# First attention's last four groups written out among the dense mixture's first blocks

## The reference

```python
h = _L0_tok_ref(x, L0_tok_w, L0_tok_b, 16)
h = h + _L0_attn_ref(_layernorm(h), ...)
h = h + _L0_ffn_ref(_layernorm(h), ...)
...
def _attention(x, w_qkv, w_proj, b_proj, ln_gamma, ln_beta):      # 8 heads of 16
    ...
    attn = jax.nn.softmax(jnp.einsum('bhnd,bhmd->bhnm', q, k) * SCALE, axis=-1)
    out = jnp.einsum('bhnm,bhmd->bhnd', attn, v)
    ...
    out = jnp.einsum('bnc,dc->bnd', out, w_proj) + b_proj
    y = x + out
    return (y - mean) / jnp.sqrt(var + 1e-05) * ln_gamma + ln_beta
...
# _L0_ffn_ref: every token goes through all 8 experts (128 -> 512 -> 128)
leaf_probs = _leaf_probs(flat_x, rw, rb)          # 7 sigmoids in a tree, 8 products
h = jnp.einsum('nd,edh->neh', flat_x, w1) + b1[None]
h = jax.nn.gelu(h, approximate=False)
y = jnp.einsum('neh,ehd->ned', h, w2) + b2[None]
out = jnp.einsum('ned,ne->nd', y, leaf_probs)
```

## Time and profile before

| | us |
|---|---|
| median of three runs | 1234.58 |
| the profiled execution | 1236.1 |
| its span, the time in which instructions ran | 1234.3 |
| PE busy in the span | 1098.2 (89%) |
| DVE, ACT, POOL busy | 904.1, 845.1, 526.2 |
| last probabilities to the start of up(5), 161.6 to 201.5 | 39.9 |
| in it PE busy | 31.87 |

### The profile page before, as it was taken

How to read it: one execution, slowest core, us unless ns; L and a number is a source line. 1 busy time by engine, 2 the same in 40 slices (tenths; PEclk the granted TensorE clock), 3 DMA queues, 4 the chain that set the end, 5 groups by cost and what they waited for, 6 DMA issues and landing times. The chain is left out here.

```text
span 1234.3 us, 29279 instructions
## 1 busy us (share of the span) xinstructions
PE 1098.2 (89%) x8508; PEld 910.6 (74%) x8508; DVE 904.1 (73%) x2770; ACT 845.1 (68%) x2821; POOL 526.2 (43%) x885
## 2 busy tenths in 40 slices
PE   8999979999998999887388599998899899869996
PEld 5778857888887788776288477786678688657884
DVE  0488847999976889956565488886899788755774
ACT  1498858888885555557243378887788499846995
POOL 0379864444304278855252653323342011034552
PEclk9999989999999999988599689999999999959997
DMA  7300002322210000001522200000333100024441
GB/s 293 96 2 3 2 1 63 110 71 65 65 43 23 1 2 1 2 1 38 195 61 50 63 14 2 11 2 2 115 113 113 34 3 2 2 80 122 131 130 36
DMA packets 50824, 66.68 MB, mean 54 GB/s; under 512 B 8100, under 2 KB 30904, under 8 KB 50552
## 3 DMA queue, kind: packets, MB, share of 16 engines
q1 hardware_dynamic: 44552, 53.39, 14.2%
q0 software_dynamic: 4432, 6.59, 2.1%
q10 hardware_dynamic: 1696, 4.98, 1.0%
HBM read 58.32 MB, written 6.71 MB: 53 GB/s over the span
## 5 line engine op out<-in xcount | busy, mean ns | idle before, releaser
L495 DVE TENSOR_TENSOR f_parts<-T,f_parts 128x512 fp32r<-128x512 f32 (+1 forms) x240 | 181.7, 796 | 21.1 <-ACT f_parts L479 19.6
L471 ACT ACTIVATE T<-quad_bank,f_b1s 128x512 f32<-128x512 f32 (+1 forms) x240 | 150.5, 648 | 43.2 <-PE quad_bank L442 34.3
L442 PE MATMUL quad_bank<-XP,f_wp 128*128 128x512 f32 (+1 forms) x720 | 165.3, 373 | 1.1 <-ACT T L471 1.1
L442 PEld LDWEIGHTS quad_bank<-XP,f_wp 128*128 128x128 f32 x720 | 125.6, 188 | 26.4 <-ACT T L471 1.4
L479 ACT ACTIVATE f_parts<-T 128x512 fp32r<-128x512 f32 (+1 forms) x240 | 132.7, 593 | 0.0
L954 ACT ACTIVATE a_late<-quad_bank,a_shift 108x108 f32<-108x108 f32 x352 | 119.1, 363 | 2.7 <-DVE a_shift L1022 2.4
L455 PE MATMUL bank<-f_parts,f_wp 128*128 128x512 f32 (+1 forms) x480 | 116.7, 379 | 4.7 <-DVE XT L504 2.0
L455 PEld LDWEIGHTS bank<-f_parts,f_wp 128*128 128x128 f32 x480 | 85.4, 192 | 23.5 <-DVE a_late L524 2.8
L384 POOL TENSOR_TENSOR f_wp<-f_ws,const 128x512 fp32r<-128x512 f32 (+1 forms) x32 | 31.0, 968 | 122.3 <-DMA f_ws<-in_f_w 53.9
L954 ACT ACTIVATION_READ_ACCUMULATOR a_late<-quad_bank,a_shift 108x1 f32 x352 | 77.2, 219 | 0.0
L765 POOL TENSOR_TENSOR a_ve<-a_mv,const 108x1 f32<-108x1 f32 x44 | 8.3, 189 | 152.1 <-DVE a_mv L1079 152.0
(11 more groups left out here) (470 smaller groups left out, 3105.9 us busy)
## 6 DMA issues: line engine op xcount, KB each, us to landing
a_late<-f_gates SPq DMA_DIRECT2D x64, 256.0 KB, 3.2
a_wqk<-in_a_wqk SPq DMA_DIRECT2D x24, 256.0 KB, 2.5
f_ws<-in_f_w SPq DMA_DIRECT2D x16, 256.0 KB, 3.8
pats<-in_patches SPq DMA_DIRECT2D x5, 648.0 KB, 10.7
pats<-in_patches ACTq DMA_DIRECT2D x5, 648.0 KB, 14.8
a_late<-f_gates SPq DMA_DIRECT2D x16, 128.0 KB, 3.6
f_w1a<-in_f_w SPq DMA_DIRECT2D x1, 2048.0 KB, 11.4
f_w2a<-in_f_w SPq DMA_DIRECT2D x1, 2048.0 KB, 16.2
```

Of the source, the lines that this page charges most:

```text
L442: mm = pe.matmul(self.m.quad_bank[:, q % 4, 0:w], self.wp[0][:, e % 2, a, c * 128:(c + 1) * 128], self.xp[:, b, t0:t0 + w], start=((a, b) ...
L471: act.activation(self.full[:, q % 4, 0:w], self.m.quad_bank[:, q % 4, 0:w], self.func, bias=self.b1s[:, e * self.chunks + c:e * self.chunk ...
L495: dve.tensor_tensor(self.lo[:, q % self.ring, 0:w], self.full[:, q % 4, 0:w], self.hi[:, q % self.ring, 0:w], ALU.subtract).then_inc(self. ...
```

## The change

The last steps of PE, ACT and DVE, from G+4 on, are replaced by one list each, `last_groups`; POOL keeps its steps. In them:

- up(0) and up(1) are cut in halves, and the turn of group 17 and the output matmul of group 21 stand between the halves of up(0), the turn of 18 between those of up(1), 19 behind down(0), 20 and 21 behind up(2).
- the turns of groups 17, 18, 19 and 21 go to PSUM bank 1, that of 20 to bank 0.
- ACT calls GELU once on one column (`first_gelu`) before its first real GELU, so that the table load stands there; `high(17)` is behind two GELUs.
- DVE adds group 21 to `yt` and does the layer norms of 20 and 21 between the low parts; `low(17)` no longer stands ahead of the add.
- the six last router tiles stand together behind down(1); the logits are taken in DVE's turn of block 2.
- the gates are made in DVE's turn of block 2 (`gates_at` = 2) and not of block 0, PE turns them behind down(3) and not down(2), ACT copies them behind block 4 and not block 3.

```diff
...
 
-    def __init__(self, nc, m, ctx, sem, name, io, bias, func, experts, chunks, gates, room, lead, aside=None):
-        self.aside = aside
+    def __init__(self, nc, m, ctx, sem, name, io, bias, func, experts, chunks, gates, room, lead, aside=None, gates_at=0):
+        self.aside, self.gates_at, self.turn_at = aside, gates_at, 1 + lead + gates_at // 2
         if aside is not None:
...
 
-    def up(self, pe, i):
+    def up(self, pe, i, chunks=None):
         e, n, t0, w = self.block(i)
...
             pe.wait_ge(self.x_split, self.groups_in((t0 + w) // 128))
-        for c in range(self.chunks):
+        for c in chunks or range(self.chunks):
             q = i * self.chunks + c
...
 
-    def lows(self, dve, i):
+    def lows(self, dve, i, chunks=None):
         e, n, t0, w = self.block(i)
-        for c in range(self.chunks):
+        for c in chunks or range(self.chunks):
             q = i * self.chunks + c
...
             self.down(pe, i)
-            if i == 1 + self.lead:
+            if i == self.turn_at:
                 turn_gates()
...
             self.hidden(act, i)
-            if i == 1 + 2 * self.lead:
+            if i == self.turn_at + self.lead:
                 act.wait_ge(self.gt_psum, 1)
...
 
-    def vector(self, dve, done):
+    def vector(self, dve, done, between={}):
 
...
             ins.then_inc(self.h_done, 1)
-        dve.wait_ge(self.lg_ready, 2)
-        self.gates_first(dve)
         for i in range(self.last):
             e, n = divmod(i, nb)
+            if i in between:
+                between[i]()
+            if i == self.gates_at:
+                dve.wait_ge(self.lg_ready, 2)
+                self.gates_first(dve)
             if done <= i + self.lead < self.last:
...
                 self.raw(dve, n)
-                if n < len(self.gates_last):
-                    self.gates_last[n](dve)
-                if n == len(self.gates_last) - 1:
+                k = n - self.gates_at
+                if 0 <= k < len(self.gates_last):
+                    self.gates_last[k](dve)
+                if k == len(self.gates_last) - 1:
                     dve.drain()
...
     joined = lambda eng, step, depth: [step(t, t % 2) for t in range(G + 8)]
-    run = joined if follow is not None or channel_stats is not None else steps
-    turned_in = lambda t: [] if follow is None or t < 9 else [t - 9] if t < G + 5 else [G - 4, G - 3] if t == G + 5 else [t - 8]
-    turned_by = lambda t: max(0, t - 8) if t < G + 5 else t - 7
+    to_last_value = lambda eng, step, depth: [step(t, t % 2) for t in range(G + 4)]
+    run = to_last_value if follow is not None else joined if channel_stats is not None else steps
+    turned_in = lambda t: [] if follow is None or t < 9 else [t - 9]
+    turned_by = lambda t: max(0, t - 8)
     with ExitStack() as ctx:
...
         lg_at = m.quad_bank[:, 3, tiles * P:512]
+        first_gelu = sb("first_gelu", [128, 1]) if follow is not None else None
         routed_by = lambda t: mix.tiles_of(turned_by(t - 1))
...
                         mix.normalise(pool, t - 7)
-            run(pool, step, depth)
+            (joined if mix is not None else run)(pool, step, depth)
             if mix is not None:
...
                     pe.wait_ge(v_ready, min(G, t - 3))
-                    if t > G + 3:
-                        pe.wait_ge(y_done, min(G, t - 5))
                     mix.turn(pe, g, turn_at(i))
...
                     mm.then_inc(o_psum, 1)
-                if mix is not None:
-                    after_step(t)
 
-            def after_step(t):
-                if t == G + 3:
-                    pe.wait_ge(exps, 2 * G)
-                    pe.wait_ge(mix.lg_ready, 1)
-                    mix.up(pe, 0)
-                if t == G + 4:
-                    mix.up(pe, 1)
-                if t == G + 5:
-                    mix.route(pe, early_tiles, 14, qkbank[0], early_tiles)
-                    mix.down(pe, 0)
-                if t == G + 6:
-                    mix.route(pe, 14, 16, qkbank[0], early_tiles)
-                    mix.up(pe, 2)
-                if t == G + 7:
-                    mix.route(pe, 16, NT, qkbank[0], early_tiles)
-                    mix.down(pe, 1)
+            def last_groups():
+                pe.wait_ge(exps, 2 * G)
+                mix.up(pe, 0, (0, 1))
+                mix.turn(pe, G - 5, qkbank[0][:, 0:P])
+                pe.wait_ge(o_done, G)
+                pe.wait_ge(y_done, G - 1)
+                pe.wait_ge(mix.x_split, G - 5)
+                pe.matmul(xbank[0:P, 0:D], oT[:, :], wo[:, :], start=True, stop=True).then_inc(y_psum, 1)
+                pe.wait_ge(mix.lg_ready, 1)
+                mix.up(pe, 0, (2, 3))
+                mix.up(pe, 1, (0, 1))
+                pe.wait_ge(mix.x_split, G - 4)
+                mix.turn(pe, G - 4, qkbank[0][:, 0:P])
+                mix.up(pe, 1, (2, 3))
+                mix.down(pe, 0)
+                pe.wait_ge(mix.x_split, G - 3)
+                mix.turn(pe, G - 3, qkbank[0][:, 0:P])
+                mix.up(pe, 2)
+                pe.wait_ge(y_done, G)
+                mix.turn(pe, G - 2, xbank[:, 0:P])
+                pe.wait_ge(mix.x_split, G - 2)
+                mix.turn(pe, G - 1, qkbank[0][:, 0:P])
+                mix.down(pe, 1)
+                mix.route(pe, early_tiles, NT, qkbank[0], early_tiles)
             run(pe, step, depth)
             if mix is not None:
+                last_groups()
                 mix.tensor(pe, 3, 2)
...
                     exponentials(t - 3, q, 1)
-                for c in range(mix.chunks if mix is not None else 0):
-                    if t in (G + 3, G + 5):
-                        mix.gelu(act, (t - G - 3) // 2, c)
-                    if t in (G + 4, G + 6):
-                        mix.gelu_high(act, (t - G - 4) // 2, c)
+
+            def last_groups():
+                act.activation(first_gelu[:, :], m.one, mix.func)
+                mix.gelu(act, 0, 0)
+                mix.gelu(act, 0, 1)
+                mix.high(act, G - 5, qkbank[0][:, 0:P], G - 4)
+                mix.gelu(act, 0, 2)
+                mix.gelu(act, 0, 3)
+                for c in range(4):
+                    mix.gelu_high(act, 0, c)
+                mix.high(act, G - 4, qkbank[0][:, 0:P], G - 3)
+                for c in range(4):
+                    mix.gelu(act, 1, c)
+                mix.high(act, G - 3, qkbank[0][:, 0:P], G - 2)
+                for c in range(4):
+                    mix.gelu_high(act, 1, c)
+                for c in range(4):
+                    mix.gelu(act, 2, c)
+                mix.high(act, G - 2, xbank[:, 0:P], G - 1)
+                mix.high(act, G - 1, qkbank[0][:, 0:P], G)
+                for c in range(4):
+                    mix.gelu_high(act, 2, c)
+                mix.hidden(act, 3)
             run(act, step, depth)
             if mix is not None:
-                mix.hidden(act, 2)
+                last_groups()
                 mix.gates_middle(act, mix.lg_ready)
-                mix.scalar(act, 3)
+                mix.scalar(act, 4)
 
...
                     dve.tensor_tensor(oT[:, :], o_at, recT[:, :], ALU.mult).then_inc(o_done, 1)
-                if mix is not None and t in (G + 4, G + 6):
-                    mix.lows(dve, (t - G - 4) // 2)
+
+            def stats_of(g):
+                dve.wait_ge(h_done, g + 1)
+                mix.stats(dve, g)
+
+            def scaled(g):
+                dve.wait_ge(post_rstd, g + 1)
+                dve.tensor_scalar(yt[:, g % 2, :], yt[:, g % 2, :], mvb[:, g % 2, 0:1], rstdb[:, g % 2, :],
+                                  ALU.subtract, ALU.mult).then_inc(post_normed, 1)
+
+            def last_groups():
+                g = G - 1
+                dve.wait_ge(y_psum, G)
+                dve.wait_ge(xres_ready, G)
+                dve.wait_ge(h_done, g - 1)
+                dve.tensor_tensor(yt[:, g % 2, :], m.XN[:, bass.ts(g, D)], xbank[0:P, 0:D], ALU.add).then_inc(y_done, 1)
+                mix.low(dve, G - 5, qkbank[0][:, 0:P], G - 4)
+                dve.wait_ge(y_done, G)
+                dve.bn_stats(bnb[:, g % 2, :], yt[:, g % 2, :]).then_inc(post_stats, 1)
+                dve.drain()
+                dve.bn_aggr(mvb[:, g % 2, :], bnb[:, g % 2, :]).then_inc(post_stats, 1)
+                scaled(G - 2)
+                stats_of(G - 3)
+                mix.lows(dve, 0, (0, 1))
+                scaled(G - 1)
+                mix.lows(dve, 0, (2, 3))
+                stats_of(G - 2)
+                mix.low(dve, G - 4, qkbank[0][:, 0:P], G - 3)
+                stats_of(G - 1)
+                mix.lows(dve, 1)
+                mix.low(dve, G - 3, qkbank[0][:, 0:P], G - 2)
+
+            def last_turned():
+                mix.low(dve, G - 2, xbank[:, 0:P], G - 1)
+                mix.low(dve, G - 1, qkbank[0][:, 0:P], G)
             run(dve, step, depth)
-            dve.wait_ge(y_done, G)
             if mix is not None:
```

(8 more changed lines are left out.)

## The result

**The changed kernel takes 1226.63 us (median of 20 runs, 1220.89 to 1230.78) against 1234.53 us (20 runs, 1228.32 to 1241.58) in the same comparison: a ratio of 0.993, interval 0.9915 to 0.9946.** That is 7.9 us, 0.64%, inside the 1% that was called no change. Two later comparisons on other chips gave 0.9921 (0.9894 to 0.9949) and 0.9944 (0.9916 to 0.9972). The forecast was 8.9 us and 1225.7. The profiled execution took 1230.08 us, its span 1228.3, mean clock 0.938; that of before 1236.1, 1234.3 and 0.938.

What follows compares the result with a forecast made beforehand. It took the seam to lose PE time by waits and half clock, the mixture behind being PE-bound. Up(5) 10.6 us sooner less 1.7 for the clock gives 8.9: 1234.58 - 8.9 = 1225.7 us, range 1221.5 to 1232.

Steps and rivals of the forecast that it cites:

- What bounded the kernel: Seam loses PE time by standing still and lower clock; mixture behind is PE-bound and keeps the gain; at most 13.8 us.
- POOL's wait for the layer norm goes: Last groups: layer norm of group 20 done near 165.5 us, so POOL's wait of 2.51 us goes.
- POOL as the engine that is never idle: Last groups: POOL's steps set the chain; XN of group 21 at 174.5 to 177.9 us, taken as 177.
- One gap of PE, of 3 us: Ahead of the turns of groups 20 and 21: one gap of 0.5 to 3.9 us stays, taken as 3.
- the signs that I named: Profile checks, among them half clock at most once in the seam, up(5) at 188 to 193 us; wrong if after 195.
- The clock, 1.7 us: Behind PE's remaining gap: a short fall to 1.2 GHz costs 1.7 us, ends 0 and 3.4.
- Table load: ACT's early GELU call: GELU can begin 1.28 us sooner, less one short call; contained in the chain, not added.
- Routing at nothing: Seam: the six router tiles cost PE the same where they stand.
- gates at nothing: Seam and after: ACT's 2.77 us wait goes, PE has work meanwhile; later gates covered at no cost before expert 2.
- Contention of expert 1's splits at nothing in the seam: Block 2's low parts beside POOL's splits: 3.4 us more on DVE, taken as 0 for PE, ends 0 and 3.
- my third rival: Behind the seam: stretched low parts and a longer clock fall give back 2 to 6 us; 1229 to 1232.5; chance 0.16.
- the fourth rival: Blocks 5 to 8: DVE becomes the mixture's bound, 14.3 us lost against 8.9 won; 1240.0 us; chance 0.04.

Runs made afterwards that it cites:

- g10: Changed kernel with down(1)'s high and low parts moved into PE's gap, ahead of the turns of groups 20 and 21: 1239.73 us, ratio 0.9924 to the kernel before.
- e3: Changed kernel with the layer norm of group 20 ahead of the add of group 21 on DVE: 1236.33 us, ratio 0.989 to the kernel before.
- e1: Kernel before the change with only the gates made, turned and copied later: 1245.46 us against 1248.95, ratio 0.998.
- e2: Changed kernel with its gates one block earlier: 1240.37 us, ratio 0.9933 to the kernel before.
- g12: g11 with PE's turn of the gates and ACT's copy of them one block later: 1225.44 us against 1235.82 for the kernel before, ratio 0.992.
- g11: g10 with the layer norm of group 20 ahead of the add of group 21 on DVE: 1239.25 us, ratio 0.9926 to the kernel before.
- g9: Changed kernel unaltered, traced a third time: 1240.28 us against 1248.47 for the kernel before, ratio 0.9944.

## Why the prediction was right, step by step

**What bounded the kernel: held.** The seam lost PE time and the mixture behind it took over most of what it won. The time fell by 7.9 us; up(5) came 7.2, 8.6 and 9.0 us sooner behind up(0) in the three traces, up(15) 6.2, 8.1 and 8.5; 8.9 was forecast.

**POOL's wait for the layer norm goes: wrong.** It fell from 2.51 to 2.09 us. I had the layer norm done at 165.5, 3.9 us behind up(0), as soon as POOL was free. It was done 4.8 us behind. It stands behind the add of group 21, which needs the output matmul, behind six matmuls of up(0), which took 2.93 us at half clock and not 1.5. Either of two things removes the wait: with up(0) at full clock and the order as it is (g10) the layer norm was done at 3.56 us and POOL never stood; with the layer norm put first and up(0) at half clock (e3) the wait was gone too, and the turn of 21 came 1.6 us sooner. So what I had wrong is the clock of up(0), which I priced at 2.4 GHz, on an order that leaves the layer norm open to it.

**POOL as the engine that is never idle: held.** Its steps were 5.78 (173.69 - 167.91), 4.4 and 1.8 us, 12.0 in all (12.4 and 11.7 in the two other traces), where I took 11.4 and had 8.9 to 12.3 as ends. The slow end was right, and for the reason given: without the low parts the chain is 9.05. With the later start `XN` of 21 came 16.87 us behind up(0), 1.5 more than I took (177 - 161.6 = 15.4).

**One gap of PE, of 3 us: held** (2.71, 2.72 and 2.12 us). Two of the signs that I named failed: PE was at half clock twice in the seam and not at most once, and up(5) "later than 195 us" would have made the forecast wrong by its own words, and it came at 195.73. With the fall of the clock in it the forecast had up(5) at 190.9 + 1.7 = 192.6. Of the 3.1 us between, 1.4 are the later start of up(0), for which I should have counted from up(0) and not on the trace's clock. The other 1.7 are the forecast's own: `XN` of 21 came 1.5 us later than I took. The same shortfall is in every trace. Counted from up(0) I had 29.3 us with the clock held and 31.0 with a fall, against 31.34 and 30.93 where it held and 32.72 where it fell: 1.6 to 2.0 us short each time. **That two traces lie at 31.0 is luck**: the fall that I had priced did not come, and covered the chain that I had too short.

**The clock, 1.7 us: right in size, but not a fixed event of this kernel.** Where it fell it cost 5.75 - 4.15 = 1.6 us. The row that I took it from gives less: six us at half clock, 5.58 of them busy, lose 2.8 us and not 3.4, and half of that is 1.4. In four of seven traces the fall did not come. An expected value of some 0.7 would have been the better term.

**Table load: held.** 1.27 us for GELU, at either clock of up(0), and 0.8 for the chain when up(0) runs at full clock. What it is worth for the chain at half clock was not measured.

**Routing at nothing: no run speaks against it; gates at nothing: nearly right, by two errors.** I let ACT's wait of 2.77 us go without a price, as PE had work meanwhile. It had, but up(4) waited 1.0 us for GELU all the same, a row that I had read and not tied to the gates: their new place won 1.0 to 1.6 us of the old seam (e1). I also priced the later gates at nothing behind the seam, and there they gave back 0.8 us of it (e1); with the gates a block earlier (e2) nothing was given back.

**Contention of expert 1's splits at nothing in the seam: held, but the cover is thin.** The low parts of block 2 took 5.4 us against 2.6 of block 1, and PE did not wait. With PE 2 us sooner (g10) it waited 1.35 us for the gates queued behind them.

**Given back behind the seam (my third rival): there, in small.** Up(5) to up(15) took 51.0 us in the first trace and 50.5 in the two others, where it took 50.0 before, most of it lost between up(12) and up(13): 1.0 and 0.5 us, for which the sum had nothing. In g12 it is 3.7. This rival priced eight stretched low parts, and 2 to 6 us with a longer fall of the clock. DVE's idle time fell from 3.3 to 2.0 us of 40, so the fourth rival (DVE as the bound) was not met; but with so little slack the waits of g12 are no surprise.

**Left open.** Why the attention's last 30 us run at half clock for 0 to 9 us from trace to trace, what sets the start of up(0), and whether any order ahead of up(0) could hold the clock; it was not tried. Whether filling the gap and leaving the gates' turn where it is (g10, g11) is faster than the changed kernel: up(15) comes 1.5 to 2.2 us sooner than in the two traces in which the clock held, and the times don't show it. Filling the gap together with the gates a block earlier, which gave nothing back, was not tried.

## What to carry to other kernels

When a wait is taken out of a chain, ask what else stands on the same engine ahead of the instruction that the next engine waits for: here the add that stood behind the removed `low(17)`, with the matmuls ahead of it at half clock, kept 2.1 of 2.5 us. Price DVE and POOL together where both work from SBUF, since each stretches the other; the chain over them is as long as their overlap makes it. When a gap of the bound engine can't be closed, look first for its own later work to put into it, and then for the next thing that was just in time, which will be late. Count a gain at a point behind the last collision, not at the end of the edited place: g12 won the most at up(5) and nothing against g9 at up(15).

## What the runs showed of the hardware

- POOL's instructions stretch beside DVE's low parts, not only DVE's beside POOL's: a root on 108 numbers 0.56 to 1.76 us, `normalise` (108x128, one SBUF input tensor) 0.80 to 1.98 and 2.73, and 0.56 and 0.80 again without low parts. DVE's own 128x512 subtraction took 0.68 alone and 1.66 in the mean beside POOL's (6.63 for four). The Trainium skill, "GPSIMD Engine Reference", section "1. Specifications", names the contention for VectorE instructions with two SBUF inputs, which this one has; these rows agree.
- The granted clock behind a gap of 2.1 to 2.7 us in two pieces, with the turn of group 20 between them, fell to 1.2 GHz in three of seven traces and stayed at 2.4 GHz in four. The same order of work had 0 to 9.3 us of half clock in the 30 us ahead of the seam. The Trainium skill, "TensorE: Matmul & The Clock Gate", section "Part 1: The HAM clock gate (the "warmup" mystery)", calls the number of slow matmuls at the start of a kernel run-variable for one and the same kernel. These traces show the same in the middle of one: a single trace of a kernel can't tell a clock effect of 1.6 us from none.
- An ACT table load took 1.28 us in every row, and the function behind it began 0.01 to 0.02 us later wherever its input was there.
